# First attention: the compressed product of four heads as one matmul of 32 rows and 512 columns

## What is computed

```python
entries = einsum('bcr,bcrh->bch', softmax(token logits), hidden)     # 4 tokens -> 1 entry: 32 entries a batch row
ck = apply_rope(rmsnorm(entries @ Wk + bk, kn_w), block_ends)        # one compressed key for all heads
cv = entries @ Wv + bv                                              # one compressed value for all heads
sc = einsum('bhsd,bcd->bhsc', q, ck) * scale                        # then causal mask, top 8 of 32, softmax -> pw
ctx_sparse = pw @ cv                                                # per head: 32 entries -> 128 channels
ctx_local  = softmax(q @ lk.T * scale, masked) @ lv                  # per head: 128 tokens -> 128 channels
out = concat((ctx_sparse + ctx_local) * 0.5) @ Wo + bo
```

## Time and profile before

| what | us |
|---|---|
| median of 3 runs (lowest, highest) | 2745.82 (2744.62, 2748.7) |
| time of the profiled execution | 2758.03 |
| its span | 2756.2 |
| PE busy in the span | 2339.5 (85%) |
| DVE busy | 1871.3 (68%) |
| ACT busy | 1590.1 (58%) |
| mean granted TensorE clock | 0.941 of full |

### The profile page before, as it was taken

The page is one execution under the profiler, slowest core; times in us unless marked ns, Lnnn a source line. Parts: engine busy times, 40 slices in busy tenths (PEclk is TensorE's granted clock), DMA queues, the critical chain, the costliest instruction groups (busy, mean ns, idle before and its releaser), DMA issues. The chain is left out here.

```text
span 2756.2 us, 50448 instructions
## 1 busy us (share of the span) xinstructions
PE 2339.5 (85%) x16399; PEld 1534.9 (56%) x16545; DVE 1871.3 (68%) x4371; ACT 1590.1 (58%) x3099; POOL 716.9 (26%) x897
## 2 busy tenths in 40 slices
PE   6999999999987567777777779889997986899994
PEld 3676766767664334444444445545555664467773
DVE  5877778777774789999999912246665775234444
ACT  3656666566653579989999921056664654123332
POOL 1121121211211112222222200011111267436664
PEclk9999999999998799989889989989999998899997
DMA  5000000000001399999999930040000012446666
GB/s 198 1 1 0 0 0 0 0 0 0 0 0 46 65 207 183 176 185 180 179 184 183 186 77 1 0 148 1 1 1 7 13 64 78 143 86 110 108 108 143
DMA packets 539447, 211.18 MB, mean 77 GB/s; under 512 B 475002, under 2 KB 533878, under 8 KB 538230
## 3 DMA queue, kind: packets, MB, share of 16 engines
q1 hardware_dynamic: 518246, 180.54, 32.6%
q0 software_dynamic: 20592, 27.98, 5.9%
q10 hardware_dynamic: 416, 0.16, 0.0%
HBM read 54.27 MB, written 36.90 MB: 33 GB/s over the span
## 5 line engine op out<-in xcount | busy, mean ns | idle before, releaser
L1753 DVE TENSOR_SCALAR_CACHE_REDUCE x_row<-x_p_s,x_nsq 128x1024 f32<-128x1024 f32 x512 | 621.7, 1270 | 22.4 <-PE x_p_s L1528 22.3
L1632 ACT ACTIVATE x_ints<-x_row,x_nb 128x2048 uint16<-128x2048 f32 x256 | 511.5, 1999 | 46.4 <-DMA x_turned<-x_ints 27.6
L1528 PE MATMUL x_p_s<-x_kT,x_qz 128*128 128x512 bf16 x929 | 299.6, 412 | 145.0 <-DVE x_row L1753 137.6
L363 POOL TENSOR_TENSOR a_rstd<-a_ssq,neghalf 128x16 f32<-128x16 f32 x32 | 126.0, 3936 | 524.7 <-DVE a_ssq L874 524.7
L1528 PEld LDWEIGHTS x_p_s<-x_kT,x_qz 128*128 128x128 bf16 x1024 | 73.6, 101 | 266.7 <-DVE x_row L1753 238.7
L1656 POOL TENSOR_SCALAR x_nb<-x_low,x_hmin 128x1 f32<-128x1 f32 x256 | 75.0, 293 | 519.5 <-DVE x_row L1753 518.2
L3277 POOL DMA_INDIRECT f_acc<-f_yt,f_ids x111 | 171.9, 1548 | 136.3 <-ACT f_yt L3442 109.6
L1562 PEld LDWEIGHTS x_p_o<-x_vi,x_turned 128*128 128x128 f16 x4096 | 143.8, 98 | 87.1 <-DMA x_turned<-x_ints 18.7
L2216 ACT COPY s_eT<-sc_p_e 128x512 f32<-128x512 f32 x192 | 112.3, 585 | 133.7 <-PE sc_p_e L2106 133.6
L1562 PE MATMUL x_p_o<-x_vi,x_turned 128*128 128x16 bf16 x4096 | 143.0, 171 | 16.9 <-DMA x_turned<-x_ints 16.6
L3367 PE MATMUL f_p_g<-f_w,f_rowsT 128*128 x444 | 151.6, 464 | 0.0
(11 more groups left out here) (479 smaller groups left out, 5337.8 us busy)
## 6 DMA issues: line engine op xcount, KB each, us to landing
f_rows<-f_spread SPq DMA_DIRECT2D x111, 136.5 KB, 2.1
f_w<-in_L_ffn_w_dram SPq DMA_DIRECT2D x2, 2816.0 KB
x_turned<-x_ints SPq DMA_TRANSPOSE x224, 4.8
f_sum<-f_acc SPq DMA_DIRECT2D x6, 512.0 KB, 7.2
f_w<-in_L_ffn_w_dram SPq DMA_DIRECT2D x2, 1408.0 KB
f_spread<-f_empty SPq DMA_DIRECT2D x17, 136.5 KB, 2.6
x_res<-in_x_dram SPq DMA_DIRECT2D x2, 1024.0 KB, 6.9
a_wq<-in_L_attn_Wq_dram SPq DMA_DIRECT2D x2, 1024.0 KB, 11.0
```

Of the source, the lines that this page charges most:

```text
L363: pool.tensor_tensor(rstd[:, hs], ssq[:, hs], core.neghalf[:, 0:NH], ALU.pow).then_inc(root_h.sem, 1)
L1528: mm = pe.matmul(p_s[n % SLOTS][:, c * BANK:(c + 1) * BANK], qz[b % 2][:, par, a, :], kT[:, a, at:at + BANK], start=True, stop=True)
L1632: act.activation(ints[k][:, :], rows[k][:, :, :].rearrange("p s n -> p (s n)"), ACT.Exp, bias=nb[:, k:k + 1], scale=-1.0, accum_out=esum[: ...
L1753: dve.tensor_scalar(rows[k][:, half, :], p_s[n % SLOTS][:, :], nsq[:, b % 2, h:h + 1], HIGHEST, ALU.mult, ALU.min, accum_out=(low if half ...
```

## The change

- `cv` is [128, 128] instead of [128, 4, 128]. ACT makes it in one copy of 128 partitions instead of four of 32. POOL's memset and ACT's wait for it fall away. Each block of 32 partitions now holds the same 32 compressed values.
- `sparse_scores` reads the queries of heads 4j to 4j+3 for row block j, so that (j, entry) and (m, token) now belong to head 4j+m. In the middle of the chain (after the turn back) column slot 4m+j then belongs to head 4j+m.
- DVE's multiplication by `rqs` reads the scales in that permuted order, through an access pattern with one dimension more.
- `psT` now has head 4g+m in row block g, slot m. The compressed product of the four heads of group g is one matmul: weights `cv` of the 32 partitions of block g, moving operand those 32 partitions of `psT` over all four slots, 512 columns. It starts the bank, and the four local products of 128 columns accumulate on it.

```diff
-        cv = sb("a0_cv", [P, G, D])
+        cv = sb("a0_cv", [P, D])
...
-            pool.memset(cv[:, :, :], 0.0).then_inc(cleared, 1)
...
-                                   qT[:, j::G, :], start=True, stop=True)
+                                   qT[:, j * NG:(j + 1) * NG, :], start=True, stop=True)
...
+                    rows_of = slice(g * NC, (g + 1) * NC)
+                    pe.matmul(p_cT[:, :], cv[rows_of, :], psT[rows_of, :, :].rearrange("p j t -> p (j t)"), start=True, stop=False)
                     for h in range(G):
-                        o = p_cT[:, h * P:(h + 1) * P]
                         at = (g * G + h) * D
-                        pe.matmul(o, raw[2][:, at:at + D], pT[g % 2][:, h, :], start=(h == 0), stop=False)
-                        mm = pe.matmul(o, cv[:, h, :], psT[:, g, :], start=False, stop=(h == G - 1))
+                        mm = pe.matmul(p_cT[:, h * P:(h + 1) * P], raw[2][:, at:at + D], pT[g % 2][:, h, :], start=False, stop=(h == G - 1))
...
-                if isinstance(b, int) and b == 0:
-                    act.wait_ge(cleared, 1)
-                for h in range(G):
-                    q = slice(NC * h, NC * (h + 1))
-                    last = act.copy(cv[q, h, :], bank[q, D:2 * D])
-                last.then_inc(proj_read.sem, 1)
+                act.copy(cv[:, :], bank[:, D:2 * D]).then_inc(proj_read.sem, 1)
...
-                dve.tensor_tensor(scm[:, :, :], scm[:, :, :], bcast(rqs[:, :], [P, NH, NC]), ALU.mult).then_inc(s_arg.sem, 1)
+                placed = scm[:, :, :].rearrange("p (m g) c -> p m g c", g=NG)
+                scales = rqs[:, :].rearrange("p (g m) -> p m g", m=G).unsqueeze(3).to_broadcast([P, G, NG, NC])
+                dve.tensor_tensor(placed, placed, scales, ALU.mult).then_inc(s_arg.sem, 1)
```

## The result

The changed kernel is slower: 2773.96 us in the median of 3 runs (2773.3 to 2779.82) against 2745.82, a ratio of 1.0093 with an interval of 1.0073 to 1.0114. The two profiled executions stand closer: 2773.96 against 2758.03 us. Timed again beside the kernel before, in more runs (first experiment), the ratio was 1.008 (1.006 to 1.010), which is 22 us; the two medians there stand 20.6 us apart. The kernel before had medians of 2745.82, 2767.7, 2750.17 and 2767.36 us in the four sets of runs of this study, so a kernel is compared only with the one before of its own set.

What follows compares the result with a forecast made beforehand. TensorE was taken to bound the first attention. Saving 3.7 us and paying 0.39 us a group for changes of form gave +1.33 us a pass, +21.2 over 16: 2745.8 + 21.2 = 2767 us, own range 2762 to 2772, whole range 2756 to 2776.

Steps and rivals of the forecast that it cites:

- TensorE bounds the stage, one for one: First attention: TensorE busy 48.44 of 49.10 us a pass; what it gains or loses counts 16 times.
- the third rival: First attention: switches cost as forecast, but waits of 0.66 us a pass shrink to nothing; +10.6 us, 2756, chance 8%.
- No columns are saved, so no time is: Each group's values: 4 x 128 = 512 columns stream as before, idle rows save nothing; gain 0.234 us a pass, 3.7 over 16.
- A change of form costs 0.38 to 0.40 us a group there and back: Around each group's 32-row matmul between 128-row neighbours: 0.09 + 0.19 + 0.10 us, taken as 0.39 a group.
- the 0.21 of the earlier trace: Loss at L2089, kernel before: 1.07 us for two streams of 0.859; read as first load 0.10, way out 0.09, staggering 0.02.
- Sum: TensorE in the first attention: four groups 8.58 against 7.25 us, +1.33 a pass, +21.2 us over 16 passes.
- a dearer switch: Rival at each group's changes of form: nothing overlaps on either side of a switch; +42 us, 2788, chance 8%.
- The other engines at nothing: First attention: ACT 0.76 us a pass less, worth 0 under idle time; DVE's multiplication, POOL's memset and head order 0.
- The smaller price from the Trainium skill: At each change of form: drain of about 128 cycles, 0.053 us instead of 0.09; +16.5 us instead of +21.2.
- Row blocks run side by side: L2089, kernel before: four row blocks of one form overlap, eight records of 0.43 us taking 1.07 together.
- the second rival: In all 64 groups the 32-row matmul runs beside its 128-row neighbours, hiding its 0.859 us; -58.7 us, 2687, chance 3%.
- the 0.09 us of groups 0 and 1: Odd extra time in groups 0 and 1 of the kernel before, counted as saved within the 0.234 us a pass.

Runs made afterwards that it cites:

- first experiment: The changed kernel as it is, timed in more rounds beside the kernel before: ratio 1.008 (1.006 to 1.010), pass 50.36 us.
- experiment 2: Changed kernel with the compressed product on all 128 rows, zero-padded values, no change of form: pass 48.91 us, ratio to before 1.0009.
- experiments 2 to 5: Changed kernel with compressed product on 128 rows: pass 48.91 us; cut in halves, four form changes a group: 51.93; halves together, two changes: 50.39; on 64 rows: 50.37.
- experiment 6: Changed kernel with 32-row matmuls of two groups paired into different banks, turn_p3 and entries moved: pass 50.25 us, ratio 1.0076 to the kernel before.
- experiments 8 and 9: Changed kernel with pairs, piece order kept, entries in a scores bank: pass 48.47 us, ratio 0.9968; then also the compressed key earlier on DVE and GpSimd: 48.33, 0.9963.

## Why the prediction was right

- *TensorE bounds the stage, one for one.* Right: the idle time of a pass is the same in both kernels, and the third rival, that the waits would shrink, fell with it. Its size was misread: of the 0.66 us, 0.23 is the matmul without a record, so the rival could have been worth 0.43 x 16 = 6.9 us at most and not 10.6.
- *No columns are saved, so no time is.* Right: full rows and a quarter of them stream alike (experiment 2), and the wide matmul in place of four narrow ones, six weight loads fewer a group, was worth 0.035 us.
- *A change of form costs 0.38 to 0.40 us a group there and back.* Right to 0.01: 0.09 in, 0.19 for the stay and the way out, 0.10 for the load after the return. The group took 2.13 us against 2.144, the pass 50.36 against 50.4, and L554's two records stand 0.53 and 0.52 us from what follows, as forecast. The rows of a later stage and of another form gave the price of this one. That the 0.21 of the earlier trace rows divides into 0.10 for the load, 0.09 for the way out and 0.02 was a reading and no measurement when it was made; the changed kernel bears out the first two.
- *Sum.* +21.2 us; measured 1.31 x 16 = 21.0 by the pass, and 22 us by the longer timing (+17 to +28 by its interval). The first median's +28 lies above the forecast's own range (2762 to 2772 us) and inside of the whole range, whose upper part was there for a dearer switch. The switch wasn't dearer: single executions scatter by more than the 7 us between +21 and +28, and the first ratio's interval, +20 to +31 us, takes in the 21. That the median of three runs still fell within the range is in part luck; the pass is the better witness.
- *The other engines at nothing.* Right for ACT (0.83 us a pass less, 13 us in sum, no effect, experiment 2), DVE and the head order.
- *The smaller price from the Trainium skill*: an estimate of +16.5 us, by the drain of some 128 cycles that "TensorE: Matmul & The Clock Gate" gives in its step-by-step section. The trace has 0.09 us lost at a change and not 0.053, and the rows were nearer. The Trainium skill's rule that changing the tiling mode drains the engine ("TensorEngine Tiling (Array Packing)", Key Properties) fits experiments 2 to 5, where time is lost at each change and none without one; that it is a drain no run shows.
- *Row blocks run side by side*: not in the change, as said against the second rival, but in experiment 6.
- Weight-load records fell by 384 (16545 to 16161), as forecast. One detail was off: in the forecast the 0.09 us of groups 0 and 1 vanish in either form; they vanish in the changed kernel, whose groups 0, 1 and 2 all take 2.04 to 2.05 us, and stay with full rows.

## What to carry to other kernels

In this kernel rows of the array were free and changes of form were not. Among float32 matmuls of 128 rows, a small contraction is better padded with zeros to 128 rows, as long as the other engines have room for the padding (here four copies of 32 partitions in place of one on ACT, which had 19 us to spare), unless so much small work is put together that the 0.39 us for going there and back is earned. It was earned when two matmuls on different row blocks followed each other directly into different banks, since they shared the stream as well. Before counting a shorter TensorE as won, look for the chain on another engine that ends just before it, and for the waits that a shared bank brings in: here that gave back half.

## What was not expected of the hardware

- The price is the same for 64 rows as for 32: passes of 50.37 and 50.36 us.
- Half of the price is not the switch but the weight load behind it. A load that otherwise runs hidden starts together with its matmul at both changes, about 0.10 us each (0.53 for 0.43 in the first record of L554, 0.99 for 0.90 in L557's eight).
- The end of a loop on TensorE's queue costs nothing while the array has matmuls to run, and shows once the queue has had to wait just before it: 0.11 us between the compressed key and the next matmul before, 0.66 and 0.39 in experiments 8 and 9.
- A pass of 49 us repeats within 0.01 us from execution to execution, while the stretch behind this stage, 1925 us long, differs by some 20 us between executions of the same code (1924 to 1946). A change to this stage is read better from its pass than from the whole time.
